# A gated cross-attention and expert layer on one core: reciprocal square roots per context, reordered batches, and channel pairs added on GpSimd from the ninth context on

## What is computed

```python
# attention: cosine similarity over channels of every position with its left neighbour, itself, its right
sim = stack([cos(emb, emb_l), cos(emb, emb), cos(emb, emb_r)])      # (B, 3, T), cos = dot / (norm * norm)
out = einsum('bit,oi->bot', unfold(feature) * repeat(sim, C), w_flat)   # three taps of 128 channels each
x = x + tanh(g_xattn) * out            # feature = layernorm(x), embedding = ctx
# experts: 8 experts of rank 16, top 2 by softmax of the router
h = einsum('nd,erd->ner', flat, A);  hw = h * w      # w: the two gates of a token
x = x + tanh(g_ffn) * einsum('ner,eor->no', hw, Bm) * SCALING     # flat = layernorm(x)
```

## Time and profile before

| | us |
|---|---|
| median of 3 runs | 271.09 (271.02 to 273.68) |
| profiled execution, its own time | 274.97 |
| its span, from the first to the last instruction | 273.2 |
| PE busy | 230.4 |
| DVE busy | 173.7 |
| ACT busy | 115.9 |
| POOL busy | 103.3 |

### The profile page before, as it was taken

The page is one execution under the profiler, slowest core; times in us unless marked ns, Lnnn a source line. Parts: engine busy times, 40 slices in busy tenths (PEclk is TensorE's granted clock), DMA queues, the critical chain, the costliest instruction groups (busy, mean ns, idle before and its releaser), DMA issues.

```text
span 273.2 us, 4570 instructions
## 1 busy us (share of the span) xinstructions
PE 230.4 (84%) x1566; PEld 140.7 (52%) x1566; DVE 173.7 (64%) x394; ACT 115.9 (42%) x211; POOL 103.3 (38%) x217
## 2 busy tenths in 40 slices
PE   4664937895885899997999997799997899999992
PEld 4563415452553465564465664365664364664661
DVE  2037326569623889728689755889744769777754
ACT  3523580385142356551374562384542164532120
POOL 2593183028209131573113454413354414322220
PEclk9955795599599799997799999999999599999999
DMA  6873600400400145250142350222140121011013
GB/s 210 293 267 131 233 0 0 154 0 5 155 0 2 77 156 191 91 181 1 77 156 100 133 206 26 79 77 89 68 156 0 78 77 79 0 77 77 5 77 154
DMA packets 14629, 26.90 MB, mean 98 GB/s; under 512 B 1678, under 2 KB 10126, under 8 KB 14606
## 3 DMA queue, kind: packets, MB, share of 16 engines
q1 hardware_dynamic: 14606, 26.61, 27.7%
HBM read 18.22 MB, written 8.39 MB: 97 GB/s over the span
## 4 chain that ended last, share of the span: by engine, by line
PE 62%; DVE 14%; POOL 13%; issue 6%; ACT 3%; DMA 1%; SPq 0%; DVEq 0%; POOLq 0%; ACTq 0%
PE conv_ps L920 24%; POOL rinv L367 12%; PE hidden_ps L946 8%; PE hidden_ps L852 6%; PE xT_ps L932 5%; DVE pt L660 4%; PE out_ps L963 3%; PE sim_ps L909 3%; PE out_ps L964 2%; PE out_ps L967 2%; DVE x L704 2%; PE xT_ps L895 2%; PE out_ps L954 1%; DMA wide<-identity 1%; DVE qp L590 1%
## 5 line engine op out<-in xcount | busy, mean ns | idle before, releaser
L920 PE MATMUL conv_ps<-pt,wT 128*128 128x512 f32 x192 | 107.5, 645 | 1.0 <-DVE pt L660 1.0
L660 DVE TENSOR_TENSOR pt<-xn,sim_ps 128x512 f32<-128x512 f32 x96 | 61.0, 678 | 8.3 <-PE sim_ps L909 8.3
L503 ACT ACTIVATE xT<-xT_ps 128x512 f32<-128x512 f32 x32 | 19.1, 597 | 61.9 <-PE xT_ps L932 61.9
L367 POOL TENSOR_TENSOR rinv<-nmax,minus_half 128x32 f32<-128x32 f32 x6 | 32.6, 5436 | 25.0 <-DVE nmax L601 25.0
L383 POOL TENSOR_TENSOR ve<-mv,eps 128x1 f32<-128x1 f32 x16 | 3.9, 244 | 97.6 <-DVE mv L676 97.6
L946 PEld LDWEIGHTS hidden_ps<-aT,xT 128*128 128x128 f32 x256 | 33.1, 190 | 10.1 <-issue 8.4
L920 PEld LDWEIGHTS conv_ps<-pt,wT 128*128 128x128 f32 x192 | 33.7, 206 | 6.1 <-issue 3.8
L946 PE MATMUL hidden_ps<-aT,xT 128*128 128x136 f32 x256 | 35.2, 280 | 1.4 <-ACT sums L468 0.9
L932 PEld LDWEIGHTS xT_ps<-wide,x 128*128 128x128 f32 x128 | 16.5, 149 | 23.2 <-issue 19.4
L852 PE MATMUL hidden_ps<-qp,onehot 128*32 128x128 f32 x512 | 22.1, 325 | 2.4 <-DVE qp L590 2.4
L932 PE MATMUL xT_ps<-wide,x 128*128 128x128 f32 x128 | 20.9, 289 | 3.8 <-DVE sim L628 2.7
(11 more groups left out here) (112 smaller groups left out, 298.9 us busy)
## 6 DMA issues: line engine op xcount, KB each, us to landing
xt<-x SPq DMA_DIRECT2D x16, 512.0 KB, 3.3
et<-ctx SPq DMA_DIRECT2D x15, 514.0 KB, 4.3
out<-x SPq DMA_DIRECT2D x15, 512.0 KB, 2.6
aT_in<-expert_aT SPq DMA_DIRECT2D x1, 544.0 KB, 6.7
bm_in<-expert_b SPq DMA_DIRECT2D x1, 512.0 KB, 4.4
out<-x SPq DMA_DIRECT2D x2, 256.0 KB, 2.0
et<-ctx SPq DMA_DIRECT2D x1, 385.5 KB
wT_in<-conv_wT SPq DMA_DIRECT2D x1, 192.0 KB, 2.3
```

The costliest lines, as they stand in the source:

```text
L367: nc.gpsimd.tensor_tensor(rinv[:, :], nmax[:, :], minus_half[:, :], ALU.pow).then_inc(rinv_done, 1)
L660: nc.vector.tensor_tensor(pt[:, i, :], xn[:, n % 2, h * HALF + t:(h + 1) * HALF + t], sim_ps[:, t, :], ALU.mult).then_inc(mod_done, 1)
L920: nc.tensor.matmul(conv_ps[h][:, :], wT[:, t * P:(t + 1) * P], pt[:, i, :], start=(t == 0), stop=(t == TAPS - 1)).then_inc(tap_done, 1)
```

## The change

- `inverse_norms` works on one context at a time, on its 8 columns (128 x 8), as soon as that context's sums have been transposed and copied, which is also per context now. `nmax`, `columns` and `rinv` get two copies, one per parity of the group. The neighbour's norms take four matmuls instead of six (the columns are ordered by chunk).
- The expert means are taken on TensorE straight from `aT_in` (8 matmuls), in place of three additions on GpSimd and one matmul.
- More dummy matmuls: 11 for 6 ahead of the first sum, and 9, 5, 2, 6 and 4 at later places of the start.
- The loops over steps are replaced by lists written out for batches 0 and 1 and a part of 2, and by a loop over whole batches behind it. GpSimd's products are those of contexts 2 to 5 (before: 1, 3, 4); the first two wait until the similarities of group 0 have been split, the other two until those of group 1 have.
- From context 8 on (`FOLDED = 8`), GpSimd adds the two halves of the channel pairs (`fold`: a 128 x 1024 addition in `qp`), and `sum_context` needs 8 matmuls instead of 16.
- Context 0 is loaded in two pieces, and the transfers of `wT_in` and `rb` start earlier.

The diff, cut to what is spoken of:

```diff
-WARM_UP = 6
+WARM_UP = 11
...
-FOLDED = 16
-
-
-SQUARES, FOLDS = {(0, 3): 4, (1, 1): 5, (1, 4): 6}, {}
-SUMS = {(0, 1): 2, (0, 2): 3, (1, 0): 4, (1, 5): 5, (2, 0): 6}
-for e in range(7, 16):
-    SQUARES[e - 6, 5] = SUMS[e - 5, 5] = e
-TURNS, NEIGHBOURS, ROWS = {(0, 3): 1}, {(0, 4): 1}, {(1, 0): 1}
-for q, (f, *_) in list(enumerate(GROUPS))[2:]:
-    TURNS[f - 2, 3 if q == 2 else 0], NEIGHBOURS[f - 2, 5 if q == 2 else 3], ROWS[f - 1, 0] = q, q, q
-
-
-ON_POOL = (1, 3, 4)
+
+SQUARED, SUMMED, TURNED = ({n: n + ahead for n in range(2, 15) if n + ahead < 16} for ahead in (6, 5, 4))
+CHAINED = {members[0] - 2: q for q, members in enumerate(GROUPS) if q >= 2}
+
+
+FOLDED = 8
+
+
+ON_POOL = (2, 3, 4, 5)
 
...
-            return 16 * (e // G + (3 if e == B - 1 else 1))
+
+            return 16 * (e // G + (3 if e == B - 1 else 1 + (e % G == 0)))
...
-                if e < B - 1:
+                if e == 0:
+                    piece(0, P, 0, 2, QUARTER + 1)
+                    piece(0, P, 2, 4, QUARTER + 1)
+                elif e < B - 1:
                     piece(0, P, 0, 4, QUARTER + 1)
...
+            sp.dma_start(wT_in[:, :], conv_wT).then_inc(conv_in, 16)
             sp.dma_start(identb[:, :], identity_bf).then_inc(identb_in, 16)
             sp.wait_ge(setup, SETUP)
             load_sel(0, sel0_in)
-            sp.dma_start(wT_in[:, :], conv_wT).then_inc(conv_in, 16)
...
-            load_x(2)
             sp.dma_start(ids[:, :], expert_ids).then_inc(ffn_in, 16)
             sp.dma_start(rb[:, :], router_b.rearrange("(a n) -> a n", a=1).to_broadcast([P, E])).then_inc(ffn_in, 16)
+            load_x(2)
...
-            def inverse_norms(q):
-                pool.wait_ge(nmax_done, q + 1)
-                if q >= 1:
-                    pool.wait_ge(rnext_done, q)
-                    pool.wait_ge(sim_done, 3 * q)
-                nc.gpsimd.tensor_tensor(rinv[:, :], nmax[:, :], minus_half[:, :], ALU.pow).then_inc(rinv_done, 1)
+            def inverse_norms(e):
+                q, b = GROUP_OF[e], SLOT_OF[e]
+                pool.wait_ge(nmax_done, e + 1)
+                if q >= 2:
+
+                    pool.wait_ge(sim_done, 3 * (q - 1))
+                nc.gpsimd.tensor_tensor(of_slot(rinv[:, q % 2, :], b), of_slot(nmax[:, q % 2, :], b),
+                                        of_slot(minus_half[:, :], b), ALU.pow).then_inc(rinv_done, 1)
 
...
-            product(1)
+
+            pool.wait_ge(split, 4)
+            product(2)
             product(3)
-            sum_means()
+            inverse_norms(1)
+            inverse_norms(2)
+            inverse_norms(3)
             feature_rstd(1)
 
-            for n in range(B):
-                for i in range(STEPS):
-                    if i == 2 and n >= 1:
-                        token_rstd(n - 1)
-                    if (n, i) in TURNS:
-                        inverse_norms(TURNS[n, i])
-                    if SQUARES.get((n, i)) in ON_POOL:
-                        product(SQUARES[n, i])
-                    if i == 4 and n + 2 < B:
-                        feature_rstd(n + 2)
-                    if i == 3 and n >= 1:
-                        weigh_experts(n - 1)
-                        hidden(n - 1)
-                    if (n, i) in FOLDS:
-                        fold(FOLDS[n, i])
-                    if n == 1 and i == 3:
-                        pool.wait_ge(bm_hi_done, 1)
-                        nc.gpsimd.tensor_tensor(bm_lo[:, :], bm[:, :], bm_hi[:, :],
-                                                ALU.subtract).then_inc(bm_lo_done, 1)
+            pool.wait_ge(split, 8)
+            product(4)
+            product(5)
+            feature_rstd(2)
+            token_rstd(0)
+            inverse_norms(4)
+            weigh_experts(0)
+            hidden(0)
+            pool.wait_ge(bm_hi_done, 1)
+            nc.gpsimd.tensor_tensor(bm_lo[:, :], bm[:, :], bm_hi[:, :], ALU.subtract).then_inc(bm_lo_done, 1)
+            inverse_norms(5)
+            feature_rstd(3)
+
+            for n in range(2, B):
+                if n in TURNED:
+                    inverse_norms(TURNED[n])
+                token_rstd(n - 1)
+                weigh_experts(n - 1)
+                hidden(n - 1)
+                if n + 2 < B:
+                    feature_rstd(n + 2)
+                if n in SQUARED:
+                    fold(SQUARED[n])
             token_rstd(B - 1)
...
-            def columns_copy(q):
-                dve.wait_ge(ctxT_done, q + 1)
+            def columns_copy(e):
+                q, b = GROUP_OF[e], SLOT_OF[e]
+                dve.wait_ge(ctxT_done, e + 1)
+                if q >= 2:
+
+                    dve.wait_ge(partial, 2 * (q - 1))
+                nc.vector.tensor_scalar(of_slot(nmax[:, q % 2, :], b), columns_ps[:, 0, :, :], COS_EPS * COS_EPS, None,
+                                        ALU.max).then_inc(nmax_done, 1)
+                nc.vector.tensor_copy(of_slot(columns[:, q % 2, 1, :], b), columns_ps[:, 1, :, :]).then_inc(columns_out, 1)
+                nc.vector.tensor_copy(of_slot(columns[:, q % 2, 0, :], b), columns_ps[:, 0, :, :]).then_inc(columns_out, 1)
+
+            def partials(q):
+                dve.wait_ge(rinv_done, GROUPS[q][-1] + 1)
+                dve.wait_ge(columns_out, 2 * (GROUPS[q][-1] + 1))
...
+            for n in range(2, B):
+                picks = pick_experts(n - 1)
+                chain = similarities(CHAINED[n]) if n in CHAINED else iter(())
+                if n > 2:
+                    residual(n - 1, 1)
+                    if n in TURNED:
+                        columns_copy(TURNED[n])
+                    for k in range(TAPS, STEPS):
+                        modulate(STEPS * n + k)
+                    finish(n - 2, 0)
+                    token_stats(n - 1, 1)
+                if n in CHAINED:
+                    take(partials(CHAINED[n]), 2)
+                if n > 2:
+                    token_variance(n - 1)
+                take(chain, 2)
+                for _ in range(3):
+                    take(picks)
+                    take(chain)
+                residual(n, 0)
+                take(chain)
+                if n + 1 < B:
+                    for k in range(TAPS):
+                        modulate(STEPS * (n + 1) + k)
+                finish(n - 2, 1)
+                token_stats(n, 0)
+                if n in SQUARED:
+                    product(SQUARED[n])
+                if n in CHAINED:
+                    rows_low(CHAINED[n])
+                hidden_rest(n - 1)
...
-
-
-                pe.wait_ge(rinv_done, q + 1)
+                pe.wait_ge(rinv_done, GROUPS[q][-1] + 1)
                 pe.wait_ge(partial, 2 * q + 1)
-                if tokens:
...
-                pe.wait_ge(summed_means, 3)
+                pe.wait_ge(aT_in_done, 16)
                 pe.wait_ge(sums_out, 4)
-                nc.tensor.matmul(h_ps, mean_w[:, :], aT_sum[:, 0, :], start=True, stop=True).then_inc(mean_w_done, 1)
+                for c in range(KC):
+                    last = nc.tensor.matmul(h_ps, mean_w[:, :], aT_in[:, c, :], start=(c == 0), stop=(c == KC - 1))
+                last.then_inc(mean_w_done, 1)
...
             pe.wait_ge(warm_set, 1)
             keep_warm(WARM_UP)
@@ -981,69 +1002,111 @@
             pe.wait_ge(onehot_done, 1)
             sum_context(0)
             keep_warm(2)
-            transpose_context(0, 0)
-            keep_warm(6)
+            transpose_context(0, 0, 0, 0)
+            keep_warm(9)
             next_norms(0, 0)
-            keep_warm(4)
+            keep_warm(5)
             pe.wait_ge(identb_in, 16)
-            transpose_similarities(0, 0)
-            sum_context(1)
+            transpose_similarities(0, 0, 1)
+            keep_warm(2)
             pe.wait_ge(sel0_in, 16 * TAPS)
             spread_similarities(0, 0)
...
+            keep_warm(4)
+            spread_similarities(1, 0)
+            sum_context(4)
+            tap(STEPS)
...
+            for n in range(3, B):
+                tokens = 2 * n - 1
+                spread_similarities(n, 1)
+                if n in TURNED:
+                    transpose_context(TURNED[n], tokens, passed, passed)
+                    turned += 1
+                experts_out(n - 2, 0)
+                tap(STEPS * n)
+                transpose_tokens(n - 1, 1, turned, passed, passed)
+                experts_in(n - 1, 0, turned)
+                tap(STEPS * n + 1)
+                experts_in(n - 1, 1)
+                if n in CHAINED:
+                    next_norms(CHAINED[n], tokens + 1)
+                tap(STEPS * n + 2)
+                if n + 1 < B:
+                    spread_similarities(n + 1, 0)
+                experts_out(n - 2, 1)
+                tap(STEPS * n + 3)
+                transpose_tokens(n, 0, turned, passed + (n in CHAINED), passed)
+                tap(STEPS * n + 4)
+                if n in CHAINED:
+                    transpose_similarities(CHAINED[n], tokens + 2, turned)
```

(5 more changed lines are left out.)

407 lines of the change are left out of this document (192 added, 215 removed).

## The result

The changed kernel takes 221.93 us (median of 4 executions, 220.93 to 227.07) and the kernel before 272.38 beside it, a ratio of 0.813 with a 95% interval of 0.802 to 0.823. The forecast was 222. The profiled execution took 221.01 us with a span of 219.2. The one execution of 227.07 ran at a lower granted clock (0.97), and the ratio leaves it out.

What follows compares the result with a forecast made beforehand. TensorE's work, broken up by the groups' powers on GpSimd at a cost in clock, was the bound. Gains of 12.2 + 8.9 + 7.9 + 4.9 + 18.1 = 52.0, plus 2 for clock, gave 222 us (range 214 to 236).

Steps and rivals of the forecast that it cites:

- The power: GpSimd's power of 8 columns, on a line between the rows for one and 32 columns: 1.67 us, bounds 0.57 and 5.44.
- The mechanism: In batch 5 the group's 5.44 us power stalls VectorE 4.78 us and TensorE 1.75, then TensorE runs at half clock.
- The start: Path up to the first tap, walked step by step: tap 0 at 15.4 us instead of 27.62, 12.2 us gained.
- Batches 0 and 1: Batch 0: 15.6 us for 24.5, 8.9 gained; batch 1: 12.5 for 20.4, 7.9 gained.
- Batch 2: GpSimd late, group's last power at 51.7; batch 17.1 us for 22.0, 4.9 gained, batch 3 starting at 60.6.
- Batches 3 to 11: 11.3 us without a chain, 13.6 with one, 13.1 for batch 11; 108.1 us for 126.2, 18.1 gained.
- The allowance for the clock: 2 us added because stops of 1.5 and 0.75 us in batches 1 and 2 may cost the clock once.
- The addition: GpSimd's addition for the sums, taken at 1.89 us, or 2.4 by the skill's rule; hidden if VectorE's two-input instructions aren't met.
- The clock: Rival: clock not up at the start; 3 to 4 us lost there, as much in batch 0; 229 us, chance 0.14.
- GpSimd in the way: Rival: additions and powers meet VectorE's two-input instructions or delay token_rstd in every batch; 13 us, 235 us, chance 0.19.
- The slower rival: Rival: 8 strided columns cost 5.44 us like 32, batches 3 to 11 last 18.6 each; about 300 us, chance 0.02.
- The break-even: Power length at which the change stops gaining: about 4.9 us, from 52 gained over 16 powers, 3.2 above 1.67.

Runs made afterwards that it cites:

- the kernel with 21 more columns: Changed kernel with a second power of 21 constant columns, read by nothing, ahead of each of the 16 powers on GpSimd: 273.52 us, ratio 1.014 to the kernel before.
- the one with the new start: Changed kernel with its start reordered: sums of contexts 1 and 2 replace dummies, second group's norms ahead of the means: 220.28 us, ratio 0.804 to the kernel before.

## Why the prediction was right, point by point

- **The power.** 1.67 us was forecast from two rows and measured at 1.67 sixteen times. The group row for 24 columns (4.18) and the 3.71 for 21 lie on the same line.
- **The mechanism.** That a group's power broke TensorE's work up is shown from both sides: 34.5 us come back when it is taken out of the kernel before, and 13 are lost when it is put back into the changed one. Its effect on the clock is a large part of both (18.0 of 40.1 us and 8.8 of 15.1 by TensorE's busy time).
- **A row of batch 5 read wrongly.** The prediction says that `token_rstd` starts at 126.26 us because it is queued behind the power. The row says otherwise: GpSimd had stood idle for 3.04 us before it and waited for VectorE's `mv`. The power had ended at 123.2. In the kernel before, the wait reached TensorE through VectorE, whose list stood at `dr` for 4.78 us and only then went on to its products, its addition and the statistics that end in `mv`. `token_rstd` stands directly behind the powers only where they are long and the batch has no chain, as in the kernel with 21 more columns. The sum takes the length of batch 5 from its window and not from this step, so it did no harm.
- **The start.** Each step of the walk came within 0.2 us, and the first tap at 15.62 for 15.4. It holds by a narrow margin: the power began 0.01 us ahead of VectorE's product. That it costs 1 us to come second was not in the walk.
- **Batches 0 and 1.** 15.7 and 11.9 us for 15.6 and 12.5.
- **Batch 2.** 18.4 for 17.1, the worst step. The last power ran from 50.52 to 52.18 and not to 51.7, and TensorE's wait for the residual (0.83) was left out. What I missed on GpSimd are its short operations beside VectorE's product: a one-column power took 1.55 for 0.56, a small selection 1.29 for 0.40 (rows below).

Rows of batches 1 and 2 of the changed kernel: GpSimd's selection and one-column power beside VectorE's products, and TensorE's two waits (the second in the row of its weight load).

```profile
42.25 1.25 DVE L607 TENSOR_TENSOR qp<-et 128x1024 f32<-128x1024 f32 x1
42.47 1.29 POOL L406 TENSOR_SCALAR ga<-ids,topf,g 128x8 f32<-128x8 f32 x1
...
48.66 1.22 DVE L607 TENSOR_TENSOR qp<-et 128x1024 f32<-128x1024 f32 x1
48.74 1.55 POOL L378 TENSOR_TENSOR rs<-ve,minus_half 128x1 f32<-128x1 f32 x1
52.50 0.38 PE L903 MATMUL xT_ps<-rinv,wide 128*128 128x32 f32 x2 [1.40 <-POOL rinv L370]
55.63 0.42 PEld L950 LDWEIGHTS xT_ps<-wide,x 128*128 128x128 f32 x4 [0.83 <-DVE x L686]
```

- **Batches 3 to 11.** 11.22 for 11.3 without a chain, and 12.76 for 13.6 with one (12.53 for 13.1 in batch 11). The 0.7 to 1.0 us that I gave for a late `rows` and `hidden_rest` is the mis-sized term: TensorE stood for 0.07 us in the whole of batch 5.
- **The allowance for the clock.** 2 us were added for a fall in batches 1 and 2, and in the profiled execution there was none. That is an accident of this execution: in the kernel without the additions and in the one with the new start TensorE had the same stop of 1.4 us in batch 2, ran there at a granted clock of 0.91, and batch 2 lasted 19.35 and 19.08 us for 18.43. With the term above it made the span 4 us too long (223.2 for 219.2), and the walk's 225.0 stands against a profiled execution of 221.0. Another error took most of that back: I scaled by 0.986 from the profiled execution to the median, as in the kernel before, while the changed kernel's profiled execution is no slower than its median. So the 222 is closer to the result than its steps are, by luck.
- **The addition.** 2.38 us each, not the 1.89 of a product, and near the 2.4 that the prediction worked out from the Trainium skill's rule (GPSIMD Engine Reference, section 4.1, Engine selection). It stayed hidden, so the sum did not change.
- **The rivals.** *The clock* was the right worry of the wrong size: with few dummies the loss is 4 us and not 7, up to 1 of it from the stretched power, and batch 0 hardly feels it. *GpSimd in the way* did not come true, but it does as soon as a power is a little longer: 15 us at 3.3 us per context. *The slower rival* was priced too high, 300 for 273.5, because it took today's batch 11 (18.6 us) for every batch; a batch without a chain lasts 12.4 to 14.0 with 5.4 us of powers, since the group's chain isn't in it. The break-even with the kernel before lies near 5.4 us per context and not at 4.9.

## What to carry to other kernels

Where an engine off the path serves several chains, ask for its longest single operation, not for its busy share: GpSimd was busy for 38% of the time, and six of its operations cost 35 us, nearly half of it as lost clock. Cut such an operation until it fits into the slack of whoever waits, and stop there; below 1.67 us the power was worth 1 us at most, and twice that cost 15 us. When two engines disturb each other, the order in which their operations start counts beside their length (1.0 us on a power of 1.67 here), and a wait or a tiny operation that fixes the order can pay for itself.

## What the chip showed that I had not expected

- **The disturbance has a direction.** A power on GpSimd that starts behind a running product of VectorE (both inputs in SBUF) takes 2.65 to 2.72 us for 1.67. In all of these rows it ends 0.14 to 0.15 us before a power would end that starts with the product's end, so it waits for nearly the whole rest of the product. One that began 0.67 us into a product (in the kernel with 21 more columns) took 2.07. A product that starts behind a running power takes 1.22 to 1.28, as without one, in every profile in which the two meet. A product on GpSimd does hold VectorE up: a cast and a subtraction took 1.95 and 1.88 for 0.24 and 0.30. The Trainium skill (SBUF — State Buffer, section SBUF: two separate sides) says that the pair of ports that the two engines share is locked by whichever operation starts first, one of GpSimd's or one of VectorE's with both inputs in SBUF or in certain modes, for its whole length. The first and the third agree; the second doesn't, for a power, and there the measurement decides. Why a power doesn't keep VectorE out is not settled here.
- **Not every operation of VectorE is caught.** Beside GpSimd's products the modulation (0.64 a piece), the copies of `rows` (0.75) and, in the versions with the new start, the subtraction for the means (1.29, and 1.28 with no product beside it), all with an input in PSUM, kept their lengths.
- **An addition isn't a product.** On GpSimd 1,024 columns took 2.38 us added in place or subtracted (`bm_lo`) and 1.89 multiplied.
- **The clock is paid in some places and not in others.** The same stall, 1.6 us of TensorE ahead of the norms, cost batch 5 of the kernel with a group's power 3.38 us and batch 8 1.86. The stop of 1.4 us in batch 2 left the clock at 1.00 in the changed kernel and took it to 0.91 in two others. What decides it was not tried.
